# A two-layer graph network on one core: features loaded once, edge vectors loaded and turned inside layer 0's loop

## The reference

```
h    = x @ W_lin.T                                 # the h table, one row per node
ef   = (softplus(basis(w) @ Wf1 + bf1) - ln 2) @ Wf2 + bf2
agg  = segment_sum(h[src] * ef, dst)
x    = layernorm(x + (softplus(agg @ Wm1 + bm1) - ln 2) @ Wm2 + bm2)

rhat = edge_vec / (norm(edge_vec) + 1e-12)         # edge_attr_3, 3 numbers per edge
w    = mlp(radial_embedding(edge_weight))          # 4 x 32 numbers per edge
m    = products of w, rhat, (x @ W_up)[src]
x    = layernorm(x + segment_sum(m, dst) @ W_out / 16)
```

## Time and profile before

| | |
|---|---|
| timed, median of 3 | 2066.67 us (2065.38 to 2067.56) |
| the profiled execution | 2057.45 us, its span 2055.7 us |
| PE busy | 1801.3 us (88%) |
| DVE busy | 1423.8 us (69%) |
| ACT busy | 634.0 us (31%) |
| POOL busy | 1499.4 us (73%) |
| mean granted clock of TensorE | 0.868 of full speed |

### The profile page before, as it was taken

One profiled execution on the slowest core, in us unless ns is written; L12 is line 12 of the kernel. 1 busy time (PEld: TensorE's weight loads), 2 busy tenths in 40 slices (PEclk: granted clock), 3 DMA queues, 4 the chain that ended last, 5 costly groups with the idle time before them and its releaser, 6 DMA issues.

```text
span 2055.7 us, 30288 instructions
## 1 busy us (share of the span) xinstructions
PE 1801.3 (88%) x10138; PEld 1347.4 (66%) x10138; DVE 1423.8 (69%) x3186; ACT 634.0 (31%) x950; POOL 1499.4 (73%) x1598
## 2 busy tenths in 40 slices
PE   5778877878788788888869999999999999999997
PEld 5566655556566566656637777776767777777776
DVE  7765555656566666666647787777777777787876
ACT  3544444444444444444341111121111111121211
POOL 4777777777777777777736777777777777777774
PEclk9687788988888888888869899899998899899999
DMA  7522322222222222223311222222222222222232
GB/s 209 146 79 80 85 80 80 80 79 80 85 78 82 79 80 79 82 78 85 111 40 52 57 58 56 57 57 56 57 57 56 57 56 57 57 58 57 57 101 54
DMA packets 105804, 153.91 MB, mean 75 GB/s; under 512 B 33982, under 2 KB 65490, under 8 KB 105546
## 3 DMA queue, kind: packets, MB, share of 16 engines
q0 software_dynamic: 50656, 103.11, 18.6%
q1 hardware_dynamic: 54652, 46.76, 7.5%
q10 hardware_dynamic: 336, 2.01, 0.3%
HBM read 138.53 MB, written 13.21 MB: 74 GB/s over the span
## 4 chain that ended last, share of the span: by engine, by line
POOL 43%; PE 35%; issue 15%; DMA 3%; DVE 1%; SPq 1%; ACT 1%; DVEq 0%; POOLq 0%; ACTq 0%
POOL sent L469 43%; PE bank L849 15%; PE bank L834 8%; PE bank L913 4%; PE bank L905 4%; PE bank L836 2%; DMA unit_in<-in_x 1%; PE bank L1018 1%; PE bank L933 1%; DMA sent<-up_table,senders 1%; ACT unit_in L657 0%; DMA radial_embedding<-basis 0%; ACT unit_in L655 0%; SPq L559 0%; PE bank L793 0%
## 5 line engine op out<-in xcount | busy, mean ns | idle before, releaser
L469 POOL DMA_INDIRECT sent<-up_table,senders x784 | 739.8, 944 | 269.9 <-issue 234.4
L469 POOL DMA_INDIRECT sent<-h_table,senders x784 | 742.8, 947 | 265.4 <-issue 238.1
L849 PE MATMUL bank<-onehot,msg 128*128 128x128 f32 x4704 | 734.0, 314 | 5.2 <-DVE msg L1260 3.2
L849 PEld LDWEIGHTS bank<-onehot,msg 128*128 128x128 f32 x4704 | 652.0, 219 | 117.4 <-issue 108.2
L834 PE MATMUL bank<-Wf_sb,hid 128*128 128x128 f32 x1568 | 260.7, 318 | 180.4 <-DVE msg L1225 180.3
L834 PEld LDWEIGHTS bank<-Wf_sb,hid 128*128 128x128 f32 x1568 | 227.9, 223 | 207.4 <-DVE msg L1225 205.5
L1225 DVE TENSOR_TENSOR msg<-bank,sent 128x512 f32<-128x512 f32 x196 | 135.6, 692 | 315.7 <-issue 270.9
L834 PEld LDWEIGHTS bank<-w_sb,h 64*128 64x128 f32 x1568 | 191.6, 189 | 172.9 <-issue 134.2
L1186 DVE TENSOR_TENSOR onehot<-relT,bank 128x512 f32<-128x512 f32 x392 | 266.7, 680 | 8.2 <-PE bank L849 6.7
L696 ACT ACTIVATE soft<-soft 128x512 f32<-128x512 f32 x196 | 123.0, 627 | 453.8 <-DVE soft L1206 453.8
L1199 DVE TENSOR_TENSOR sums<-sums,bank 128x128 f32 (+1 forms) x392 | 137.1, 350 | 178.8 <-PE bank L849 175.6
(11 more groups left out here) (144 smaller groups left out, 1430.1 us busy)
## 6 DMA issues: line engine op xcount, KB each, us to landing
basis<-in_edge_weight SPq DMA_DIRECT2D x196, 100.0 KB
sent<-h_table,senders POOLq DMA_INDIRECT x784
sent<-up_table,senders POOLq DMA_INDIRECT x784
basis<-near_lengths SPq DMA_DIRECT2D x196, 16.0 KB
radial_embedding<-basis SPq DMA_DIRECT2D x196, 16.0 KB
emb_in<-radial_embedding SPq DMA_DIRECT2D x98, 32.0 KB
unit_in<-in_x SPq DMA_DIRECT2D x12, 256.0 KB, 3.8
h_table<-h SPq DMA_DIRECT2D x12, 256.0 KB, 3.0
```

Of the source, the lines that this page charges most:

```text
L469: pool.indirect_dma_start(sent[:, n % SLOTS, j, :], None, table, bass.IndirectOffsetOnAxis(pick, 0))\
L849: last = t_.matmul(ps[:, k, :], msg[:, p, j, k * P:(k + 1) * P], onehot[:, p, j, :], start=(j == 0), stop=(j == HALF_CHUNKS - 1))
```

## The change

x is loaded once, unit by unit, to its place in `x_sb`, with a semaphore per unit; the slots of `unit_in` are not used for it, and `load_features` of the loop is gone. SP issues all loads, then all stores; `src_i` is loaded behind the second unit. PE turns the senders behind unit 6, not ahead of the units. The receivers are not turned for the branch that is taken. The edge vectors are loaded by ACT's queue in its step 0 of layer 0; PE turns them in six parts at its steps 8 to 13, DVE copies them in its steps 9 to 14, ACT squares them in step 15, DVE sums the squares in step 17, ACT takes the root in step 17, and DVE does reciprocals (into a PSUM bank, in two parts) and products in step 20. POOL clears the sums in 13 pieces, behind its loads. `windows_iota` is made in the branch that is not taken.

```
 SP (sync)
-        def load_and_store(back):
-            u, b = back(0), back(4)
-            if u is not None:
-                wait(sp, table0["turned"], u.upto(WIDE))
-                rows = x[at(u.tile(P), u.cols), :]
-                sp.dma_start(unit_in[0:u.rows, u.wide_slot, 0:u.tiles, :], ...)
-            if b is not None:
-                store_table(table0, h_dram, b)
+        for u in units:
+            load_features(u)          # x_sb, d_x[u]; src_i behind u == 1
+        for u in units:
+            store_table(table0, h_dram, u)
+            if u.rel == len(units) - 3:
+                sp.wait_ge(s_near, 1)
+                sp.dma_start(near_dram.rearrange("(g a) e -> g (a e)", a=2), wt_rows)\
+                    .then_inc(d_near, 16)
...
-            if h.counter.eng is None and h.pair() < FEATURE_LOADS:
-                load_features(h.pair())
-                if h.pair() == FEATURE_LOADS - 1:
-                    load_layer1_weights()
+            if h.rel == 6:
+                load_layer1_weights()

 POOL (gpsimd)
+        for first in range(0, width, HALF):
+            g.memset(sums[:, 0, first:min(first + HALF, width)], 0.0).then_inc(s_cleared, 1)

 ACT (scalar)
-        act.dma_start(attr, edge_attr.rearrange("(g e) c -> g (e c)", e=PAIR))\
-            .then_inc(d_rows[3], 16)
...
+        def copy_product(sm, u):
+            wait(act, sm["product"], u.upto())
+            wait(act, sm["stored"][u.wide_slot], u.rel // WIDE * 16)
+            a.activation(rows_out[u.wide_slot][0:u.rows, 0:u.tiles, :], ...)
...
+            if h.rel == 0:
+                act.dma_start(attr, edge_attr.rearrange("(g e) c -> g (e c)", e=PAIR))\
+                    .then_inc(d_rows[3], 16)
+            if ways_at(h) == 7:
+                act.wait_ge(s_ways_copied, 6)
+                a.activation(squares, dir_columns, ACT.Square).then_inc(s_norm, 1)

 PE (tensor)
-        pe.wait_ge(s_dve, 1)
-        turn_all(src_f)
...
+        for u in units:
+            turn_unit(table0, u)
+            if u.rel >= 1:
+                product_unit(table0, units[u.rel - 1], W_linT)
+            if u.rel == 6:
+                pe.wait_ge(s_dve, 1)
+                turn_all(src_f)
...
+        def turn_ways(part):
+            c, first = part // 2, part % 2 * 4
+            if part == 0:
+                pe.wait_ge(d_rows[3], 16)
+            wait(pe, s_ways_copied, part)
+            for j in range(first, first + 4):
+                last = t_.transpose(quads[3][:, j - first, 0:pairs],
+                                    attr[:, j * P * 3 + c:((j + 1) * P - 1) * 3 + c + 1:3],
+                                    ident[0:pairs, 0:pairs])
+            last.then_inc(s_ways_turned, 1)
...
         def layer0(h):
+            if ways_at(h) is not None and ways_at(h) < 6:
+                turn_ways(ways_at(h))

 DVE (vector)
-        then(v.memset(sums[:, 0, :], 0.0))
...
-        copy_turn(dstT)
-        for c in range(3):
-            copy_turn(dirT[:, :, :, c])
...
+        def copy_way(part):
+            c, first = part // 2, part % 2 * 4
+            dve.wait_ge(s_ways_turned, part + 1)
+            v.tensor_copy(dirT[:, :, first:first + 4, c].rearrange("p g j -> p j g"),
+                          quads[3][:, :, 0:pairs]).then_inc(s_ways_copied, 1)
...
         def layer0(h, base):
-            if h.counter.eng is None and h.rel in (5, 6):
-                squared_lengths(h.rel - 5)
-            if h.rel in (12, 14):
-                unit_directions(h.rel // 2 - 6)
+            if ways_at(h) is not None and 1 <= ways_at(h) < 7:
+                copy_way(ways_at(h) - 1)
+            if ways_at(h) == 9:
+                lengths()
+            if ways_at(h) == 12:
+                unit_directions()
```

More of the change, by code:

```diff
@@ L121, in all_halves, with for_halves @@
         step(Half(n, count))
-def for_halves(eng, iterations, step, behind):
+def for_halves(eng, iterations, step, behind, alone=()):
     count = iterations * SLOTS
[L128 to L135, removed]
+    written = sorted(set(range(min(2, iterations))) | set(alone))
+    for n, here in enumerate(written):
+        for i in range(here * SLOTS, (here + 1) * SLOTS):
+            step(Half(i, count))
+        end = (written + [iterations])[n + 1]
+        if end > here + 1:
+            with eng.Fori(here + 1, end) as it:
+                counter = Counter(eng, it)
+                for s in range(SLOTS):
+                    step(Half(s, count, counter))
     for n in range(count, count + behind):
@@ L380, in stores_of, with ways_at @@
     def stores_of(slot):
[L382 removed]
+        return 16 * (last_unit // WIDE + (slot <= last_unit % WIDE))
+    def ways_at(h):
+        return h.rel - 8 if h.counter.eng is None and 8 <= h.rel < 8 + 14 else None
     def early_at(n):
@@ L516, in _ @@
         wt_halves = edge_weight.rearrange("(n e) -> n e", e=HALF)
[L518 to L525, removed]
-            if piece == 0 and nodes % P:
-                sp.dma_start(x_sb[0:nodes % P, whole, :], x[whole * P:nodes, :]).then_inc(d_x, 16)
         def load_layer1_weights():
@@ L620, in _, with copy_turned @@
         a.activation(W_linT[:], bank[6][:, 0:P], ACT.Copy).then_inc(s_wTc, 1)
[L622 to L639 removed]
+        def copy_turned(sm, u):
+            wait(act, sm["turned"], u.upto())
+            wait(act, sm["product"], u.upto(2))
+            a.activation(unit_T[:, u.slot, 0:u.cols], bank[u.slot][:, 0:u.cols], ACT.Copy)\
+                .then_inc(sm["copied"], 1)
+        def copy_product(sm, u):
+            wait(act, sm["product"], u.upto())
+            wait(act, sm["stored"][u.wide_slot], u.rel // WIDE * 16)
+            a.activation(rows_out[u.wide_slot][0:u.rows, 0:u.tiles, :],
+                         quads[2 + u.slot][0:u.rows, 0:u.tiles, :], ACT.Copy)\
+                .then_inc(sm["ready"], 1)
+        for n in range(len(units) + 2):
+            if n < len(units):
+                copy_turned(table0, units[n])
+            if n >= 2:
+                copy_product(table0, units[n - 2])
         a.preload_act_table_set("natural_log_exp_and_others")
@@ L1045, in layer0_any @@
         def layer0_any(h):
+            if ways_at(h) == 0:
+                for part in range(6):
+                    turn_ways(part)
             if h.parity == 0:
@@ L1403, in units_any @@
         def units_any():
-            for part in range(2):
-                unit_directions(part)
             output_weights()
@@ L1532, in layer0_any @@
         def layer0_any(h):
-            if h.counter.eng is None and h.rel == 0:
-                for part in range(2):
-                    squared_lengths(part)
+            if ways_at(h) == 0:
+                for part in range(6):
+                    copy_way(part)
+            if ways_at(h) == 9:
+                lengths()
+            if ways_at(h) == 13:
+                unit_directions()
             cap0(h)
@@ L1552, in _ @@
         with dve.Else():
+            steps[0] = own_steps
+            copy_turn(dstT)
+            for k in range(all_windows):
+                last = v.tensor_scalar(windows_iota[:, k * WINDOW:(k + 1) * WINDOW], iota[:],
+                                       float(k * WINDOW), None, ALU.add)
+            then(last)
             for u in units:
```

127 lines of the change are left out of this document (47 added, 80 removed).

## The result

The changed kernel took 2052.07 us (median of seven runs, 2045.77 to 2059.74) against 2065.38 us for the kernel before (seven, 2061.37 to 2067.56): a ratio of 0.9934, with a 95% interval of 0.9917 to 0.9952, or 13.3 us by the medians. Measured twice more, each time beside the kernel before on one chip, the same kernel gave 0.9954 [0.9938, 0.9970] and 0.9968 [0.9952, 0.9983]. By the medians the three gains are 13.3, 9.4 and 6.6 us. So the question is also which of these microseconds the program saves every time. The kernel before took 2065.38 us beside this measurement, not the 2066.67 that the forecast started from; 1.3 of the 6.8 us are that.

A forecast was written before the change was run, and what follows sets the result against it. Layer 0 was taken as bound by POOL's gather stream, so the first gather's 7.8 us earlier start was the whole gain: 2066.67 to 2058.9 us. Own range 2056.5 to 2060.5; with rivals 2054 to 2065.

The forecast's parts named there:

- The squaring goes to ACT ... count nothing: Layer 0 loop: moving the 2.60 us squaring from VectorE to ACT changes the time by nothing.
- a stream of gathers with a fixed beat: Layer 0: 783 gather steps of 1.252 us each, so it ends 980 us after its start unless messages delay it.
- The first gather: End of set-up: first gather starts at 37.4 us instead of 45.2, 7.8 earlier, between 6.4 and 9.3.
- the tail: Set-up, from ACT's last product copy to the first gather: 3.8 us, chosen between 3.2 and 5.18.
- stores behind loads: Rival, set-up: stores wait for the loads, first gather at 40 to 43 us, gain about 3.2, 2063.5 us; chance 0.16.
- The consumers: Basis, filter, message: first basis load 4.1 us earlier, message 0 ends at 56.0 before gather 16 needs it at 57.4.
- The 1.2 MB of edge vectors cross the first basis loads: Start of layer 0: this load meets the basis loads, where 3.2 MB of features did before; no cost was charged.
- The copies in steps 9 to 14: Layer 0: VectorE's edge-vector copies, 1.06 us each, bring steps to about 4.4 us, hidden below four gathers' 5.0.
- the step with the reciprocals: Layer 0: reciprocal, product and a small addition share one VectorE step of some 8.3 us; nothing was charged.
- The clock rival: Rival: PE stays at 1.2 GHz through the loop's turns, about 13 us lost, 5 more than gained, 2072 us; chance 0.05.
- the port rival: Rival, set-up: POOL's memsets block VectorE's chain through shared ports, chain 5.4 us later, gain 3.8, 2062.9 us; chance 0.04.

The follow-up runs named there:

- before_ports: Kernel before with only two changes: squares taken by ACT in its step 0, reciprocals put to PSUM in two halves; 2063.3 us, ratio 0.9972.
- ports_undone: Changed kernel with squares on VectorE again and reciprocals in SBUF, so that the product has both inputs there; 2061.62 us, ratio 0.9977 to the kernel before.
- third_after: The changed kernel, unchanged, measured a third time beside the kernel before; 2060.05 us, ratio 0.9968.
- attr4: Changed kernel with the edge vectors' load issued in ACT's step 4 of layer 0 instead of step 0; 2061.11 us, ratio 0.9979 to the kernel before.
- again_before: The kernel before, unchanged, measured again against itself for a second trace; 2065.85 us, ratio 0.9996.
- again_after: The changed kernel, unchanged, measured a second time for a second trace; 2056.94 us, ratio 0.9954 to the kernel before.

## Why the prediction was wrong in size

**The step that failed** is the one of the loop: "The squaring goes to ACT ... count nothing", and "nothing" again for the reciprocal and the product. With it fell "a stream of gathers with a fixed beat". VectorE's time there is hidden, as argued. What was missed is that an instruction of another engine stood still beside it. The gathers are the stream that ends the layer, and two of them were stretched by 2.85 us; the edit of operands removes that (before_ports) and its reverse brings it back (ports_undone). This term alone does not take the time out of the forecast's range; the end of this section adds up the rest. The forecast even gave the beat as a mean of 783 steps, 1.252 us; a mean cannot show two steps that are long. The Trainium skill, "SBUF — State Buffer", section "SBUF: two separate sides", lists beside the faster modes a VectorE instruction with two SBUF inputs as one that takes the shared ports, against a GpSimd instruction that reads SBUF. The forecast weighed that section for the memset alone. These traces agree with it for the gathers: with two SBUF inputs 2.25 to 3.16 us, with one of them in PSUM 0.94.

**The first gather: mechanism right, 1.1 to 3.6 us too early.** ACT's fifth product copy did wait for the first store, which stands behind all the loads, and ended that wait at 22.33, forecast 23.3. ACT in after:

```profile
22.33 0.60 ACT L624 ACTIVATE h<-bank 128x512 f32<-128x512 f32 x1 [3.75 <-DMA h_table<-h]
...
31.23 0.76 ACT L624 ACTIVATE h<-bank 128x512 f32<-128x512 f32 x2 [0.49 <-PE bank L795]
```

The last copies end at 31.99, forecast 33.6. The term that was mis-sized is the tail from there: 3.8 was taken, between 3.2 and 5.18, and it is 38.46 - 31.99 = 6.47, outside both ends. SP issues the last two stores from 31.86 to 33.56, behind the near lengths, which the change moved ahead of them; for that the forecast took 3.8 and not 3.2. The store just ahead of the near lengths landed 2.5 us after its issue and the one just behind them 4.5 (2.4 and 4.5 in third_after). SP in after, and the landing of these two stores:

```profile
31.17 0.54 SPq L517 DMA_DIRECT2D near_lengths<-wt_space  x1
31.86 1.70 SPq L507 DMA_DIRECT2D h_table<-h  x2
```

```profile
DMA to landing us min/median/max: 2.5/2.5/2.5
DMA to landing us min/median/max: 4.5/4.5/4.5
```

No run moves the near lengths back, so that they make the tail longer is read from these rows and not shown by an edit.

The rest is TensorE. In third_after the fifth copy starts at 22.3 as well, and the last copies end at 34.52, 2.53 later; the tail is the same 6.46. PE's next product, and then the windows (us, busy of PE, PEld, DVE, ACT, POOL, granted clock, DMA share, GB/s), each of after first and of third_after second:

```profile
23.07 1.13 PE L795 MATMUL bank<-W_linT,unit_T 128*128 128x128 f32 x8 [3.11 <-ACT h L624]
23.01 2.05 PE L795 MATMUL bank<-W_linT,unit_T 128*128 128x128 f32 x8 [2.99 <-ACT h L624]
```

```profile
22.00:28.00 6.00, 4.93 (x43) 4.81 (x44) 5.63 (x11) 4.24 (x8) 0.00 (x0) 1.00 0.60 174
22.00:28.00 6.00, 4.99 (x23) 5.02 (x24) 5.64 (x11) 2.66 (x5) 0.00 (x0) 0.50 0.47 135
```

In both PE had stood for 3 us, waiting for the copy that waited for the store. Behind that wait the granted clock was 1.00 (the level of 2.4 GHz) in one trace and 0.50 (1.2 GHz) in the other, and the same eight pieces took 1.13 and 2.05 us. What decides between the two stays open. In three traces the first gather starts at 38.46, 39.64 and 40.98, a mean of 39.69 against 45.58 in two traces of before: 5.9 us, where 7.8 was forecast. The 40.98 crosses the forecast's own sign for stores behind loads, "a first gather after 40", but the first store was not late in it; the tail and the clock were.

**The consumers: on time, with the wrong message as the margin.** The weights' cast ended at 38.29 (forecast 39.6), the first basis load was issued at 40.32 (41.4), message 0 ended at 54.46 (56.0). But it was message 1 that a gather waited for. SP and ACT in after show why:

```profile
40.32 0.44 SPq L556 DMA_DIRECT2D basis<-in_edge_weight  x1
...
45.95 0.61 SPq L566 DMA_DIRECT2D radial_embedding<-basis  x2
53.42 0.29 SPq L556 DMA_DIRECT2D basis<-in_edge_weight  x1
```

```profile
44.36 0.72 ACT L679 ACTIVATE basis<-basis,neg_centers 122x512 f32<-122x512 f32 x1 [10.57 <-DMA basis<-near_lengths]
45.12 0.32 ACTq L702 DMA_DIRECT2D sums<-in_edge_attr  x1
...
56.73 0.72 ACT L679 ACTIVATE basis<-basis,neg_centers 122x512 f32<-122x512 f32 x1 [5.20 <-DMA basis<-near_lengths]
```

The forecast had "The 1.2 MB of edge vectors cross the first basis loads", and left it there. In fact the load is issued at 45.12, just ahead of the first stores of the radial embedding at 45.95, and the next basis loads, into the buffers that these stores empty, are issued only at 53.42. ACT makes its bases in order, and the third, for halves 4 and 5, waited 5.20 us, to 56.73. Exp and Ln of half 1 itself were over by then (51.52). But PE makes the hidden layer of halves 4 and 5 ahead of the filter of half 1, and VectorE waits for Ln of half 2, which stands behind that basis on ACT, ahead of message 1. PE and DVE in after:

```profile
58.35 2.08 PE L885 MATMUL bank<-basis,Wf_sb 50*128 50x256 f32 x8 [4.65 <-ACT basis L682]
60.36 2.06 PE L833 MATMUL bank<-Wf_sb,hid 128*128 128x128 f32 x8
```

```profile
59.67 0.75 DVE L1216 SCALAR_TENSOR_TENSOR hid<-bank,cols,soft 128x512 f32<-128x512 f32 x1 [5.21 <-ACT soft L691]
...
62.77 0.69 DVE L1226 TENSOR_TENSOR msg<-bank,sent 128x512 f32<-128x512 f32 x1 [0.90 <-PE bank L835]
```

So message 1 comes 9.0 us behind message 0. With the edge vectors in step 4, SP issues these loads at 49.61 and message 1 starts at 59.87 (attr4). In the traces of after the wait is small, 0.2 and 1.6 us beyond the gap of 0.3 in two and none in the third, because the gathers were later than forecast as well. Had the first gather come at 37.4, gather 20 would have wanted message 1 at 62.4, 1.0 before it ended.

**What held.** The copies in steps 9 to 14 cost nothing (messages at 83.34 and 86.94, 3.6 us a step against four gathers' 5.0), nor did the step with the reciprocals, 8.9 us from 121.77 to 130.63. No DVE instruction of 5 us is left in the set-up. The last gather of layer 0 is at 1016.29, forecast near 1018. The clock rival did not come: no gather behind message 1 waits in the first 150 us. Nor did the port rival: the memsets took 5.93 us on POOL from 12.69, and DVE stood waiting for PE's turn of the senders until 19.22. (The cast that the forecast has end with POOL's iota ended 0.54 behind it, at 10.02 against 9.48; the 2.6 us by which it was longer stand.)

**The rest of the first measurement.** The two terms that the program fixes, by means over the traces: first gather 5.9, gathers of layer 0 978.25 against 981.24, so 3.0 (the long gathers alone cost 2.85 and 3.2); together 8.9 us. Put into the forecast's sum they give 2066.67 - 8.9 = 2057.8, which lies inside its range, as do the two later medians, 2056.94 and 2060.05. That is luck: 1.9 us too much for the first gather and 3.0 too little for the loop largely cancel. The 2052.07 of the first measurement are 5.7 below that sum: 1.3 is the kernel before, and 4.4 has no term of the program behind it.

The three measured gains, 13.3, 9.4 and 6.6 us, have a mean of 9.8. In the traces the rest lies in the stretches that both kernels have alike. The passage runs from the last gather of layer 0 to the first of layer 1; the last column is the granted clock in the 50 us that follow it:

| trace | passage | clock in it | layer 1 | its waits for messages | clock, first 50 us |
|---|---|---|---|---|---|
| before | 28.35 | 0.75 | 1001.65 | 8.1 | 0.70 |
| again_before | 28.13 | 0.71 | 1008.95 | 15.0 | 0.69 |
| after | 24.83 | 0.84 | 1002.88 | 9.4 | 0.69 |
| again_after | 30.17 | 0.62 | 1009.03 | 12.4 | 0.58 |
| third_after | 28.35 | 0.74 | 1007.21 | 14.5 | 0.60 |

The shortest passage has the highest clock and the longest the lowest. The windows of the passage in after, then in again_after:

```profile
1016.29:1041.12 24.83, 15.59 (x80) 11.14 (x79) 13.22 (x42) 12.43 (x25) 0.94 (x1) 0.84 0.15 31
1018.90:1049.07 30.17, 18.41 (x65) 12.27 (x64) 12.01 (x36) 13.43 (x27) 0.94 (x1) 0.62 0.12 26
```

Half of the difference in layer 1 (between after and again_after) or more of it is in its gathers' waits for messages, the longest of which fall in its first 50 us; the clock of those 50 us does not order them. So after's first trace had a high clock in the passage and a short passage; its 2045.77 us are the lowest of all times of this kernel. They go up to 2064.52. The range of the forecast left this out: it was made from the uncertainty of its terms alone. What decides the clock in the passage, whether it is the cause of its length, and why the first seven runs had a lower median than the 21 later ones, stays open.

## What to carry to other kernels

Where one engine's stream sets the end, list its longest instructions and not only their mean, and look at what runs beside each long one: an operand moved to PSUM can be worth as much as a rearranged load. A stream that starts earlier is worth it only as far as the next buffer's consumer allows, so work out the margin for each of the first few halves, with every transfer that crosses their loads. And before a difference of half a per cent is explained, measure how far two traces of the same program are apart in stretches that the change does not touch. Cut those stretches at the same events, not at the same times.

## What of the hardware was not expected

A GpSimd gather of 0.94 us took 2.25 to 3.16 us beside one VectorE product of 2.60 us with both inputs in SBUF, and stayed at 0.94 beside a reciprocal of 5.05 us with one. It took 1.23 us beside a one-input instruction of 0.56 us. Each of the stretched gathers ended some 0.82 us after the VectorE instruction. A store of 256 KB issued just behind the near lengths landed 4.5 us after its issue, the one just ahead of them 2.5. In three traces of one program the passage between the layers took 24.8 to 30.2 us, with a granted clock of TensorE between 0.84 and 0.62.
